# Attention: column halves of the value products take alternate runs of 64 queries

## The reference, cut to what matters

```python
q = jnp.einsum('qdh,bcd->bhcq', Q, x) * sq
k = jnp.einsum('qdh,bcd->bhcq', K, x) * sq
v = jnp.einsum('vdh,bcd->bhcv', V, x) * sv
att = jnp.einsum('bhcq,bhCq->bhcC', q, k) / d_query
att = jnp.where(causal, att, -jnp.inf)
p = jax.nn.softmax(att, axis=-1)
y = jnp.einsum('bhcC,bhCv->bhcv', p, v)
z = jnp.einsum('dvh,bhcv->bcd', W, y) * (math.sqrt(d_embed / d_value) / num_heads)
```

## Time and profile before

| | |
|---|---|
| time, median of 3 runs | 2157.16 us (2157.01 to 2158.93) |
| span of the profiled execution (the only time recorded for it) | 2175.0 us |
| instructions | 39196 |
| PE busy | 1914.6 us (88%) |
| DVE busy | 1363.2 us (63%) |
| POOL busy | 1176.4 us (54%) |
| ACT busy | 1078.0 us (50%) |
| mean granted TensorE clock | 0.939 of full speed |

### The profile page before, as it was taken

How to read it: one execution, slowest core, us unless ns; L and a number is a source line. 1 busy time by engine, 2 the same in 40 slices (tenths; PEclk the granted TensorE clock), 3 DMA queues, 4 the chain that set the end, 5 groups by cost and what they waited for, 6 DMA issues and landing times. The chain is left out here.

```text
span 2175.0 us, 39196 instructions
## 1 busy us (share of the span) xinstructions
PE 1914.6 (88%) x11815; PEld 1434.9 (66%) x11816; DVE 1363.2 (63%) x3652; ACT 1078.0 (50%) x2250; POOL 1176.4 (54%) x1159
## 2 busy tenths in 40 slices
PE   5752999999689999999999999999999999974870
PEld 3451888888566677677777777777677777752750
DVE  7765344444367777656777656777656777653763
ACT  6321333334355555646655646555646555521760
POOL 4354232323216665536587836587836587835782
PEclk9855999999889999999999999999999999986995
DMA  9852533333331211112121102121102121122979
GB/s 337 266 170 76 126 51 51 51 51 51 80 92 50 57 47 53 55 27 58 46 74 50 48 24 61 41 56 48 50 23 59 43 57 48 41 93 60 204 131 256
DMA packets 215680, 177.29 MB, mean 82 GB/s; under 512 B 85442, under 2 KB 200727, under 8 KB 214880
## 3 DMA queue, kind: packets, MB, share of 16 engines
q1 hardware_dynamic: 177904, 138.78, 21.7%
q0 software_dynamic: 28656, 27.61, 8.3%
q10 hardware_dynamic: 8960, 8.92, 1.2%
HBM read 95.05 MB, written 80.72 MB: 81 GB/s over the span
## 5 line engine op out<-in xcount | busy, mean ns | idle before, releaser
L952 POOL TENSOR_TENSOR c_den_late<-c_den_late,c_p 128x512 f32<-128x512 f32 (+3 forms) x384 | 409.9, 1067 | 239.5 <-ACT c_p L1267 196.2
L1267 ACT ACTIVATE c_p<-PS 128x512 f32<-128x512 f32 (+3 forms) x768 | 343.0, 491 | 217.9 <-PE PS L2483 128.1
L2504 PE MATMUL PS<-c_p,c_vh 128*64 128x256 f32 (+1 forms) x2816 | 319.4, 347 | 0.0
L2452 PE MATMUL PS<-c_k,c_q 128*128 128x512 f32 (+2 forms) x768 | 289.2, 377 | 12.0 <-DVE c_max L1838 5.2
L2475 PE MATMUL PS<-c_q,c_k 128*128 128x512 f32 (+2 forms) x768 | 283.3, 373 | 2.6 <-DMA c_q<-c_mr 1.8
L2504 PEld LDWEIGHTS PS<-c_p,c_vh 128*64 128x64 f32 x2816 | 202.9, 136 | 101.5 <-issue 38.2
L888 POOL DMA_INDIRECT acc<-b_y,b_tok x71 | 110.5, 1557 | 281.5 <-ACT b_y L1137 255.0
L2476 PE MATMUL PS<-c_q,c_k 128*128 128x512 f32 (+2 forms) x768 | 258.6, 348 | 0.0
L1258 ACT ACTIVATE c_q<-PS 64x512 fp32r<-64x512 f32 x256 | 151.0, 590 | 206.8 <-PE PS L2439 191.5
L1845 DVE CUSTOM_DVE_ANT_0 PS<-PS,c_maskq,c_max 128x128 f32<-128x128 f32 (+3 forms) x256 | 143.1, 559 | 115.9 <-PE PS L2452 80.8
L1838 DVE TENSOR_REDUCE c_max<-PS 128x1 f32<-128x512 f32 x256 | 174.9, 683 | 56.3 <-PE PS L2452 53.9
(11 more groups left out here) (304 smaller groups left out, 4004.4 us busy)
## 6 DMA issues: line engine op xcount, KB each, us to landing
c_vh<-c_v SPq DMA_DIRECT2D x64, 256.0 KB
c_rrow<-rden SPq DMA_DIRECT2D x63, 256.0 KB, 3.6
routed<-b_empty SPq DMA_DIRECT2D x32, 289.0 KB, 9.2
d_xe<-routed SPq DMA_DIRECT2D x32, 289.0 KB
b_xt<-routed SPq DMA_DIRECT2D x71, 130.0 KB
b_w12T<-in_w12T_dram SPq DMA_DIRECT2D x16, 512.0 KB, 13.6
d_acc<-acc SPq DMA_DIRECT2D x16, 512.0 KB, 8.6
c_st_hi<-wqk_split SPq DMA_DIRECT2D x48, 128.0 KB
```

Source lines behind the costliest of these rows:

```text
L952: pool.tensor_tensor(den[:, off:], den[:, off:], p, ALU.add).then_inc(s_cPa, 1)
L1267: act.activation(c_p[:, P_AT[h][m]:P_AT[h][m] + WIDTH[m]], PS[:, ST_BANK[m % STB], skip:skip + WIDTH[m]], ACT.Exp, scale=ATT_SCALE).then_i ...
L2452: pe.matmul(PS[:, 2 + use[0], 0:max(w, 256)], c_q1[h][:, t * P:(t + 1) * P], c_k1[h][:, c * 512:c * 512 + max(w, 256)], start=True, stop=T ...
L2504: ins = pe.matmul(dst, c_vh[h][:, j, :], moving, start=(j == 0), stop=(t0 == 2 + a))
```

## The change

It assigns the queries to the two column halves in another way. Of each 128 queries a = 0 takes the first 64 and a = 1 the last 64. Each half then takes half of whatever width the block has: 256, 192, 128, 64 columns for widths 512, 384, 256, 128. `take_y` puts the runs of 64 back in their order.

```diff
@@ take_y
                 for a in range(2):
-                    dst = yT[h * DQ:(h + 1) * DQ, c * 512:(c + 1) * 512].rearrange("p (n a q) -> p n a q", n=2, a=2)[:, :, a, :]
-                    act.activation(dst, PS[a * DQ:(a + 1) * DQ, 6 + c, 0:256].rearrange("p (n q) -> p n q", n=2),
+                    dst = yT[h * DQ:(h + 1) * DQ, c * 512:(c + 1) * 512].rearrange("p (t a q) -> p t a q", a=2, q=DQ)[:, :, a, :]
+                    act.activation(dst, PS[a * DQ:(a + 1) * DQ, 6 + c, 0:256].rearrange("p (t q) -> p t q", q=DQ),
                                    ACT.Copy).then_inc(s_cyn, 1)
@@ outputs
                 pe.wait_ge(s_cP, H * len(BLOCKS) + (m + 1 + STB))
+                columns = c_p[:, P_AT[h][m]:P_AT[h][m] + WIDTH[m]].rearrange("p (t a q) -> p t a q", a=2, q=DQ)
                 for a in range(2):
-                    tiles = [t for t in (a, a + 2) if t >= t0]
-                    if not tiles:
-                        continue
-                    first, n = (tiles[0] - t0), len(tiles)
-                    if n == 2:
-                        at = P_AT[h][m] + first * P
-                        moving = c_p[:, at:at + 3 * P].rearrange("p (n q) -> p n q", n=3)[:, 0:3:2, :]
-                        dst = PS[a * DQ:(a + 1) * DQ, 6 + c, 0:256].rearrange("p (n q) -> p n q", n=2)
-                    else:
-                        moving = c_p[:, P_AT[h][m] + first * P:P_AT[h][m] + (first + 1) * P]
-                        dst = PS[a * DQ:(a + 1) * DQ, 6 + c, P:2 * P]
-                    ins = pe.matmul(dst, c_vh[h][:, j, :], moving, start=(j == 0), stop=(t0 == 2 + a))
+                    dst = PS[a * DQ:(a + 1) * DQ, 6 + c, t0 * DQ:4 * DQ].rearrange("p (t q) -> p t q", q=DQ)
+                    ins = pe.matmul(dst, c_vh[h][:, j, :], columns[:, :, a, :], start=(j == 0), stop=(t0 == 3))
                 ins.then_inc(s_cPu, 1)
```

## The result

| | median | range | runs |
|---|---|---|---|
| before | 2158.05 us | 2157.01 to 2161.95 | 4 |
| after | 2141.19 us | 2137.20 to 2142.67 | 4 |

The ratio is 0.9914, with a 95% interval of 0.9899 to 0.9929: 16.9 us less, between 15.3 and 21.8. The forecast was 25.7 us less, a median of 2131.5 us in a range of 2128 to 2145. The direction is right and the median lies in the range. The gain is two thirds of the forecast, and 2141 us lies above 2136, the bound beyond which the prediction itself calls the forecast wrong.

What follows compares the result with a forecast made beforehand. The prediction took PE to bound the attention: 26.8 us of PE time saved, less 1.1 us lost to waits on DVE's maxima, is 25.7 us, so 2157.2 - 25.7 = 2131.5 us, range 2128 to 2145.

Steps and rivals of the forecast that it cites:

- PE sets the pace of the attention: In the attention the other engines wait for PE, busy 1254.9 of 1272 us and idle only 3.5 us for DVE.
- A round's cost, its two queues and the sizes of the passes: Products with values: halves run side by side, the longer counts; 0.16 us fixed, 0.215 per 256-column pass, 0.161 per 192.
- The 64-column pass at 0.056 us: Last block of rounds 0 and 2: two such passes per half replace two of 0.1075 us, saving 0.103 us.
- The floor: Rival: a 64-column pass takes as long as a 128-column one, held by its weight load; gain 13.2 us; chance 0.07.
- issue: Rival: last block's passes issue at 36 ns each, four in 0.142 us; gain 22.0 us, time 2135.2; chance 0.05.
- Breaks cost nothing, and the copies of y are covered: Shorter runs in PE's moving operand and ACT's 0.378 us copies add 0; the slower rival, costly breaks, had 0.05.
- 127 x 0.211 = 26.8 us: PE time saved in the products with values: 0.211 us in each round 0 and 2, the last not counted.
- 4% of it is lost, 1.1 us: Score weight loads wait 52.5 of 1272 us for DVE's maxima, so 4% of the gain was taken as lost there.
- The rival of DVE: Next head's score products: a faster PE only waits longer for DVE's maxima; gain 0, time 2157; chance 0.04.

Runs made afterwards that it cites:

- the two halves of the change alone: Kernel before with the new query division only in c = 0 (round 0), or only in c = 1 (round 2): ratios to before 0.9948 and 0.9962.
- The three comparisons of the new division: Changed kernel against before, the same again, and the changed kernel with alternate runs of 16 queries instead of 64: ratios 0.9914, 0.9931, 0.9911.
- mark_later: Changed kernel with two steps of DVE's routing, marks and counts, one place later: attention stretch 1256.4 us, ratio to before 0.9951.

## Why the prediction was right or wrong

- *PE sets the pace of the attention*: right for most heads, and wrong as a statement on all of them. The row that I went by showed PE idle for DVE only 3.5 us; with all rows for DVE it is 7.0 of 1269 us. Such rows are an account of what is, and do not say how much slack DVE has at each place.
- *A round's cost, its two queues and the sizes of the passes*: right. 1.24 us forecast, 1.24 measured; round 1 unchanged at 1.88.
- *The 64-column pass at 0.056 us*: right. The floor (1.34) and issue (1.27) did not come about. In the trace the second pass of 64 columns starts 0.056 us behind the first in each half. The Trainium skill, page "TensorE: Matmul & The Clock Gate", section "Wait — 56ns, not 53.3ns?", has 62 ns for each matmul with hardware decode off, which by my estimate would give 1.41 us; the trace, at 28 ns for each, does not show that bound. No run here shows how matmuls are decoded.
- *Breaks cost nothing, and the copies of y are covered*: right, shown down to runs of 16 bytes.
- *127 x 0.211 = 26.8 us*: right as PE's own saving. Its busy time from the first product to the last fell by 26.2 us.
- *4% of it is lost, 1.1 us*: this is the step that failed. The term was mis-sized: 8.0 us measured, 30%. I took the share of time in which weight loads waited for DVE as the share of the gain that would be lost. The one does not give the other. A gain of 0.21 us is lost whole where another engine's chain already stands level with PE, and in part where it is less than 0.21 us ahead, and such places can have no idle time of PE in the trace at all, as behind round 0 of head 8. At three kinds of places more than the gain of one round was lost, since the chain of the other engine reached back over more than one shortened round; the two halves of the change alone showed this.
- *The rival of DVE* had the mechanism with the wrong extent. I had it for all or nothing, at 0.04.
- *The range* of 2128 to 2145 held by luck. It was made wide enough for the floor and for issue, and neither came about. The cause that did had a chance of 0.04 and was priced at a gain of 0.
- The three comparisons of the new division give 16.9, 16.8 and 19.3 us for the 18.8 us of the attention. The second, with 12.0 to 18.3, does not reach 18.8. What the rest is stays open; from the last product to the end the profiles take between 253 and 260 us with the same code.

## What to carry to other kernels

When an engine that is 99% busy gets shorter work, price the loss place by place: for each shortened piece, look at the next point where that engine waits for another, and at how much time lies between that other's finish and the wait. Pieces without that much slack give less or nothing, and two pieces inside one chain of the other engine give nothing together. Read the time at which the other engine finishes, and not PE's idle time. The length that a step of DVE has beside POOL says more on where to put it than its length alone; moving one such step was worth 8 us here, half as much as the change itself.

## What the runs showed of the hardware

- DVE operations with two inputs in SBUF stretch beside POOL's additions to three and four times their length: 0.69 to 2.21 us (L1905), 0.43 to 1.27 us (L1821), 0.18 to 0.73 us (L1782). In head 8 L1905 ends 0.55 to 0.57 us behind POOL's addition, in three batches of four kernels. DVE's maxima out of PSUM (L1838) keep 0.63 to 0.69 us everywhere.
- It goes the other way too: in `mark_later` POOL's addition of 128x256 beside L1857 took 1.52 us and ended 0.59 us behind it, where the median of such additions is 0.74.
- PE reads a float32 moving operand in runs of 4 elements (16 bytes) at the rate of long runs, 1.88 us for 16 passes of 256 columns, and ACT writes such runs at the same rate, 0.378 us for 256.
- Two column halves of the array keep queues of their own: passes of unequal width go side by side, and only the longer half counts. In the round 0 of before that starts at 1150.06 us, a = 0 starts its first pass of block j = 2 at 0.700 us and a = 1 its second pass of block j = 1 at 0.705, so one half does not wait for the other. Passes of 64 columns with a load of 64 weight columns each go at about 0.056 us in each half, (1.24 - 0.16 - 2 x 0.215 - 2 x 0.161 - 2 x 0.1075) / 2, that is 28 ns a pass over both.
